# Three feature tiles a batch in the first edge pass, outputs from batch 18 on, the work between the layers in batches 25 to 51

## The reference

```
xn = layernorm(x)
def gat_conv(x, W, attn_l, attn_r):                  # H heads of D
    feat = (x @ W).reshape(n, H, D)
    el, er = (feat * attn_l).sum(-1), (feat * attn_r).sum(-1)
    e = leaky_relu(el[src] + er[dst], 0.2)
    ex = exp(e - segment_max(e, dst)[dst])
    return segment_sum(ex / segment_sum(ex, dst)[dst] * feat[src], dst)
gnn = gat_conv(elu(gat_conv(xn, W1, ...)), W2, ...)  # 8 heads of 64, then 1 head of 256

q, k, v = xn Wq, xn Wk, xn Wv                         # 8 heads of 32
q, k = elu(q) + 1, elu(k) + 1
mix = (q @ (k^T v)) / (q . sum(k)) @ Wproj + bproj    # linear attention over all nodes

x = x + gnn + mix
return x + experts(layernorm(x))                      # 8 experts, three products each, softmax gate
```

## Time and profile before

| | us |
|---|---|
| median of 3 runs | 3120.95 (3120.32 to 3121.43) |
| profiled execution | 3122.36 |
| its span | 3120.6 |
| busy in the span: PE, DVE, ACT, POOL | 2114.3, 2182.2, 1945.9, 2079.6 |

### The profile page before, as it was taken

One profiled execution on the slowest core, in us unless ns is written; L12 is line 12 of the kernel. 1 busy time (PEld: TensorE's weight loads), 2 busy tenths in 40 slices (PEclk: granted clock), 3 DMA queues, 4 the chain that ended last, 5 costly groups with the idle time before them and its releaser, 6 DMA issues. The chain is left out here.

```text
span 3120.6 us, 33304 instructions
## 1 busy us (share of the span) xinstructions
PE 2114.3 (68%) x7086; PEld 1324.1 (42%) x7086; DVE 2182.2 (70%) x5347; ACT 1945.9 (62%) x6385; POOL 2079.6 (67%) x1989
## 2 busy tenths in 40 slices
PE   6730455555555455657666101899999999999999
PEld 4520233333333333444444100565555555655565
DVE  7481799999998987888887245567666666666531
ACT  5610788888887677778776233566666666666532
POOL 4236777777777767777773477777777777777300
PEclk9965667667675566777676555999999999999999
DMA  7432899999999999999996377666666666666400
GB/s 231 133 56 70 316 372 368 380 379 371 372 358 375 369 356 325 335 334 331 343 325 214 104 233 233 196 214 207 220 200 213 215 212 211 219 207 212 140 21 13
DMA packets 242215, 779.00 MB, mean 250 GB/s; under 512 B 69152, under 2 KB 117109, under 8 KB 215357
## 3 DMA queue, kind: packets, MB, share of 16 engines
q0 software_dynamic: 124960, 364.74, 36.8%
q1 hardware_dynamic: 103886, 398.85, 34.3%
q10 hardware_dynamic: 13167, 13.29, 1.6%
HBM read 399.48 MB, written 378.12 MB: 249 GB/s over the span
## 5 line engine op out<-in xcount | busy, mean ns | idle before, releaser
L1910 POOL DMA_INDIRECT e_rows<-scratch_table,k_src x1664 | 1730.6, 1040 | 518.0 <-issue 354.0
L2043 ACT ACTIVATE e_rows<-e_rows 128x64 f32<-128x64 f32 (+1 forms) x4160 | 1193.7, 371 | 3.4
L2020 DVE SCALAR_TENSOR_TENSOR e_ring<-e_ring,k_same,e_rows 128x520 f32<-128x520 f32 (+1 forms) x1560 | 965.7, 619 | 267.0 <-ACT e_rows L2043 189.4
L2446 PE MATMUL e_p_y<-e_wfo,e_h 128*121 128x256 f32 x1664 | 388.2, 388 | 27.9 <-DVE e_y L2232 27.9
L2446 PEld LDWEIGHTS e_p_y<-e_wfo,e_h 128*121 128x121 f32 x1664 | 310.5, 188 | 123.6 <-issue 60.5
L2420 PE MATMUL e_p_a<-e_xt,e_wf 128*128 128x484 f32 x832 | 357.9, 573 | 0.7 <-ACT e_xt L2374 0.7
L2432 PE MATMUL e_p_b<-e_h,e_wf 128*128 128x484 f32 x832 | 357.3, 572 | 0.0
L2359 ACT ACTIVATE e_h<-e_p_a,e_shift,e_scale 128x484 f32<-128x484 f32 x208 | 154.8, 751 | 227.6 <-PE e_p_a L2420 227.4
L1115 PE MATMUL e_p_kv<-e_wkv,nd_feat 128*121 128x512 f32 x208 | 188.8, 1061 | 116.5 <-DVE nd_feat L1018 116.4
L2232 DVE SCALAR_TENSOR_TENSOR e_y<-e_p_y,e_w,e_y 121x256 f32<-121x256 f32 x416 | 180.8, 476 | 101.2 <-PE e_p_y L2446 100.9
L1989 DVE TENSOR_TENSOR e_rows<-e_rows,e_shared 128x4096 f32<-128x4096 f32 x52 | 229.7, 4418 | 21.3 <-ACT e_rows L2036 21.1
(11 more groups left out here) (426 smaller groups left out, 3325.2 us busy)
## 6 DMA issues: line engine op xcount, KB each, us to landing
scratch_rows_a<-e_ring SPq DMA_DIRECT2D x104, 2112.0 KB
scratch_rows_b<-e_ring SPq DMA_DIRECT2D x104, 1032.0 KB
e_rows<-scratch_table,k_src POOLq DMA_INDIRECT x1664
scratch_table<-na_frow ACTq DMA_DIRECT2D x52, 245.8 KB
scratch_table<-nd_feat SPq DMA_DIRECT2D x52, 124.8 KB
na_x<-in_x SPq DMA_DIRECT2D x13, 484.0 KB
e_wkv<-in_x SPq DMA_DIRECT2D x52, 121.0 KB
scratch_res<-e_wkv SPq DMA_DIRECT2D x52, 121.0 KB
```

The lines of the kernel that those rows point to most:

```text
L1910: nc.gpsimd.indirect_dma_start(out=rows[:, n % B, g, :], out_offset=None, in_=table, in_offset=bass.IndirectOffsetOnAxis(ap=k.src[:, n * G ...
L2020: nc.vector.scalar_tensor_tensor(ring[:, i, j - c0, 0:W + H], prev, k.same[:, n * G + j:n * G + j + 1], rows[:, rb, j, 0:W + H], ALU.mult, ...
L2043: last = nc.scalar.activation(rows[:, rb, j, at], rows[:, rb, j, at], ACT.Copy, scale=rows[:, rb, j, W + h:W + h + 1])
L2446: last = nc.tensor.matmul(self.p_y[bank][0:BK, i * D:(i + 1) * D], self.h2[:, e % 2, kt, v:v + BK], self.wfo[:, e, kt, :], start=kt == 0, ...
```

## The change

Features are worked out three tiles a batch in 18 batches (17 with three, the last with one); the outputs take batches 18 to 43, and batches 44 to 51 have neither features nor outputs. The work between the layers starts at batch 25 and has one or two tiles a batch, which start at steps 2 and 12 (in the last batch 2 and 7). The steps of the features move: ACT's parts stand after steps 2, 7 and 12, DVE's before steps 4, 9 and 14. The number of tiles of each kind is the same as before, and so are 46 tiles in the batches and six behind them.

```diff
-    HALF = NB // 2
+    EACH = 3
+    HALF = -(-NB // EACH)
+    OVER = HALF + NB // 2
...
     def tiles(self, n):
-        n = n % self.HALF
-        return (2 * n, 2 * n + 1)
+        if n < self.HALF:
+            return list(range(self.EACH * n, min(self.EACH * (n + 1), NB)))
+        n -= self.HALF
+        return [2 * n, 2 * n + 1] if n < NB // 2 else []
...
     def vector(self, dve, n, j):
-        t0, t1 = self.tiles(n)
         if n < self.HALF:
-            if j == 6:
-                self.features(dve, t0)
-            if j == 13:
-                self.features(dve, t1)
-        else:
+            for i, t in enumerate(self.tiles(n)):
+                if j == 4 + 5 * i:
+                    self.features(dve, t)
+        elif n < self.OVER:
+            t0, t1 = self.tiles(n)
...
     def scalar(self, act, n, j):
-        t0, t1 = self.tiles(n)
         if n < self.HALF:
-            if j == 4:
-                self.exponents(act, t0)
-            if j == 11:
-                self.exponents(act, t1)
-        else:
+            for i, t in enumerate(self.tiles(n)):
+                if j == 2 + 5 * i:
+                    self.exponents(act, t)
+        elif n < self.OVER:
+            t0, t1 = self.tiles(n)
...
             if n < self.HALF:
...
+                for i, t in enumerate(self.tiles(n)):
+                    self.project(pe, t)
+                    if i == 0 and q is not None:
+                        tails.tensor_turn(pe, q)
+                        tails.tensor_back(pe, q)
+                    if i == 0 and q1 is not None:
+                        tails.tensor_spread(pe, q1)
+                    if i == 1 and q is not None:
+                        tails.tensor_sum(pe, q)
+                    self.context(pe, t)
...
+START = Mixing.HALF + 7
...
-    FIRST = (33, 34, 35, 36, 37, 38, 40, 41)
-    TILES = {33: 1, 34: 2, 35: 2, 36: 3, 37: 3, 38: 2, 39: 3, 40: 3, 41: 2, 42: 3, 43: 3, 44: 2, 45: 3, 46: 3, 47: 2, 48: 3,
-             49: 2, 50: 2, 51: 2}
+    FIRST = tuple(START + i for i in (0, 1, 2, 3, 4, 5, 7, 8))
+    TILES = {n: 1 if (n - START) % 10 in (0, 4, 7) else 2 for n in range(START, NB)}
-    SLOT = [2 * i if n in (34, 35) else i for n, tiles in TILES.items() for i in range(tiles)]
+    SLOT = [(2 if n < NB - 1 else 1) * i for n, tiles in TILES.items() for i in range(tiles)]
...
-    OWN = 42
+    OWN = START + 9
```

More of the change, by code:

```diff
@@ L981, in sync @@
     def sync(self, sp, n, half):
-        t = self.tiles(n)[half]
         if half == 0:
@@ L986, in sync @@
             self.load_input(sp, half)
-        if n >= self.HALF:
+        if self.HALF <= n < self.OVER:
+            t = self.tiles(n)[half]
             sp.wait_ge(self.res_ready, t + 1)
@@ L1171, in tensor @@
             if n < self.HALF:
[L1172 to L1182, removed]
-            else:
-                self.weigh(pe, t0)
+                for i, t in enumerate(self.tiles(n)):
[8 more added lines that the diff above has]
+                    self.context(pe, t)
+            else:
+                tiles = self.tiles(n)
+                if tiles:
+                    self.weigh(pe, tiles[0])
                 hidden.transposes(pe, n - 1, 2)
@@ L1187, in tensor @@
                     tails.tensor_turn(pe, q)
-                self.turn_back(pe, t0)
+                if tiles:
+                    self.turn_back(pe, tiles[0])
                 if q1 is not None:
@@ L1192, in tensor @@
                     tails.tensor_back(pe, q)
-                self.output(pe, t0)
+                if tiles:
+                    self.output(pe, tiles[0])
                 hidden.product(pe, n - 1, 2)
-                self.weigh(pe, t1)
+                if tiles:
+                    self.weigh(pe, tiles[1])
                 hidden.transposes(pe, n, 0)
@@ L1198, in tensor @@
                     tails.tensor_sum(pe, q)
-                self.turn_back(pe, t1)
-                self.output(pe, t1)
+                if tiles:
+                    self.turn_back(pe, tiles[1])
+                    self.output(pe, tiles[1])
                 hidden.product(pe, n, 0)
@@ L1289, in __init__ @@
         self.late_ht = flat[:, at:at + 8 * BK].rearrange("p (i n) -> p i n", i=2)
-        assert (self.OWN - NB // 2) * 2 * 2 * BK >= at + 8 * BK
+        assert (self.OWN - Mixing.HALF) * 2 * 2 * BK >= at + 8 * BK
         self.place()
@@ L1343, in sync @@
         a, m = self.a, self.mixing
-        if n == 30:
+        if n == Mixing.HALF + 4:
             sp.wait_ge(m.ad_ready, self.free_tiles(4 * (D + 16) + 2 * D))
@@ L1453, in vector @@
     def vector(self, dve, n, j):
-        if n == 31 and j in (1, 2, 4, 6, 8):
+        if n == Mixing.HALF + 5 and j in (1, 2, 4, 6, 8):
             self.weights(dve, j)
```

## The result

The changed kernel takes 3207.36 us (median of 4 runs, 3204.18 to 3208.19) against 3121.19 for the kernel before beside it (4 runs, 3120.32 to 3121.64): a ratio of 1.0275, 95% interval 1.0257 to 1.0292. It is slower. The span of the profiled execution is 3206.4 us.

What follows compares the result with a forecast made beforehand. Bounds: POOL without free time in feature batches, and a DVE, PE, ACT loop around one feature tile. Stages 517 + 182 + 555 + 194 + 112 = 1560 us against 1466.5, +93.5, give 3214; range 3160 to 3250.

Steps and rivals of the forecast that it cites:

- 18 feature batches: Layer one's edge pass, batches 0 to 17: 17 x 29.0 + 24 = 517 us, replacing 615.7 but for eight batches less.
- outputs alone: Batches 18 to 24 repeat batches 26 to 32 of before, same parts and same place in the period: 182.0 us.
- hidden tiles alone: Batches 44 to 50: POOL issues 140 times, 197 us at 1.405 or 175 at 1.25; 194 taken, DVE waiting for rows.
- P: Time of PE's `project` for one feature tile: taken at 4.7 us, with 3.0 and 5.5 as ends.
- tight intervals: Times between successive L1018 in a feature batch, set by the DVE, PE, ACT loop: two a batch, P + 3.92 us each.
- period of four batches: Feature batches' recurring extras: 0.3 us for DVE's wait for ACT, 0.3 for scans, 0.8 for carries and merge, per batch.
- POOL cannot make it up: POOL's issues all remain, so waits in feature batches cannot be regained later: 17 x (29.0 - 23.7) = 90 us idle.
- The explanation by ports: Gathers take 0.94 us beside L1989, 1.42 beside L2020's two-SBUF-input sums; by that rule batches 44 to 50 cost 197 us.
- The third tile nearly free: Rival, feature batches: ACT does the third tile while it now waits for PE, 24.6 us a batch; 3105 us, 4%.
- The high clock: Rival, feature batches: PE's long rests go, a project takes 3.8 us, 27.2 a batch, the 18 take 486; 3183 us, 16%.
- POOL not binding behind the features: Rival, after the feature batches: hidden tiles alone cost 175 us, the batches before them 535; 3175 us, 14%.
- Slower still: Rival: P = 5.5 in feature batches (+27) and the output batches keep 30.8 us a batch (+30); 3271 us, 6%.

Runs made afterwards that it cites:

- The features alone: Kernel before with only three feature tiles a batch in batches 0 to 17, outputs and hidden tiles by the old table, batches 18 to 25 empty: 3206.22 us, ratio 1.0276.

## Why the prediction was right

The forecast was 3214 us, +93.5; it is 3207.4, +86. The terms, in its order:

| stage | predicted | measured |
|---|---|---|
| 18 feature batches | 517 | 512.0 |
| outputs alone | 182 | 184.6 |
| outputs and hidden tiles | 555 | 557.9 |
| hidden tiles alone | 194 | 188.1 |
| last batch and drain | 112 | 110.6 |

**Features: the mechanism is shown, the length of an ordinary batch within 1%.** An ordinary batch takes 28.85 us (17 of them 490.4) against 29.0, the last 21.6 against 24. Two steps inside it missed in opposite directions. P was taken at 4.7, and PE's groups of after give less (batches 1 to 17, 49 tiles):

```profile
L1117 PE MATMUL e_p_kv<-e_wkv,nd_feat 128*121 128x512 f32 x196 | 160.2, 964 | 66.5 <-DVE nd_feat L1022 66.5
L1120 PE MATMUL e_p_q<-nd_feat,e_early 128*128 128x121 f32 x392 | 63.4, 315 | 0.0
```

(160.2 + 63.4) / 49 - 0.20 = 4.36; single projects run from 2.9 to 5.5 us. The granted clock did rise, from 0.68 in the first 18 batches of before to 0.72. Against that, the 32 tight intervals of tiles 3 to 50 last 9.05 in the mean, not P + 3.92 = 8.3: the work on the carries between two features doesn't fall into spare time, as I took it to, but stands in the loop, as at 722.13 above. Without its project such an interval lasts 3.9 to 4.2 us in the two batches of a period that have no carries, 4.4 in the mean in the second, and 5.2 and 6.2 in the first. This is part of the 1.4 us that the forecast added for a period of four batches; by these means that part should have been 1.9 (28.85 - 18.2 - 2 x 4.36). That P was 0.34 too high, twice a batch, and this part 0.5 too low is luck: the two nearly cancel.

**POOL cannot make it up: right.** Predicted were 90 us of idle POOL, measured 99. Its gathers gave 14 back, which leaves 85: over 18 batches POOL is busy for 320.9 us instead of 335.0, since a gather takes 1.061 instead of 1.126 us when fewer begin inside a sum (80 of 281 issues in batches 1 to 17, 158 of 414 before). The features alone make the same loss, and eight empty batches cost 188 us.

**Outputs alone: 2.6 more than the 182.0 copied over.** The stage lasts as long as before within 1.5%; the copy was a fair price.

**Hidden tiles alone: the term that was mis-sized.** It was to be between POOL's 175 and 197, and I took 194. It is 188.1, since POOL's 143.4 and 129 gaps of 0.305 are 183 us. It issued 129 times there and not 140, because it used up a lead: in batch 44 its gathers started 4.4 us in the mean behind the sums that free their rows, in batch 49 it was 13.2. DVE's waits for rows, 9.5 us, come in batches 47 and 50 alone. The floor of issues was drawn from the first batch on, as if nothing had been ahead. The price of a gather in that stage, 1.095 us, is what the term said (1.10). The stages together were forecast 6.8 us too long, with errors of both signs.

**The explanation by ports.** The two rows that I weighed (0.94 beside L1989, 1.42 beside the sums) pointed the right way: the gathers stayed long with small stores and became short with short sums. By the rule of the Trainium skill ("SBUF — State Buffer", section "Who interferes with whom"), that a DVE instruction with two SBUF inputs contends with a GpSimd instruction that reads SBUF, the trace agrees: 157 of 158 gathers are held by a sum that they begin inside, and none of 76 by L1989. That a gather costs 1.42 beside sums was too simple, though, as not every gather beside them is held: it depends on how much of the sum is left when it begins. So a sum of 257 columns, which has two SBUF inputs as well, costs a gather almost nothing in the mean.

**The rivals.** The third tile nearly free (3105) is out in this kernel: its tight intervals last 7.4 to 10.2 us, 9.05 in the mean. It was also priced too low: with P = 3.0 the forecast's own terms give 18.2 + 6.0 + 1.4 = 25.6 us a batch, and the 24.6 that it uses has no working. With the second pair of tiles it is nearly free, and still gives no gain, since the balance point of 23.5 a batch is also POOL's price. The high clock (3183) was half true: P came down by 0.5 us of the 1.06 that it needed, and the carries in the loop took that back. POOL not binding behind the features (3175) took 175 and 535 for two stages that took 188.1 and 557.9; what spoke for it, that DVE was not seen to wait for rows, was wrong by two waits (7.1 and 6.2 us). Slower still (3271) needed P at 5.5.

## What to carry to other kernels

Where one engine's fixed work per batch fills the batch, packing other work into fewer batches saves nothing, because the emptied ones cost the same; it can only lose, if the packed ones become longer. Before work is packed, count the closed loops through a single buffer: with one PSUM pair a tile cost a whole round through DVE, PE and ACT (9 us), with two it cost nothing behind a full POOL, and the doubling is worth a try before the packing. To tell a full engine from one that merely keeps pace, add a known number of its smallest instructions: the run becomes longer by their price (1.25 us each) or not at all.

## What the runs showed of the hardware

- An indirect gather's issue on POOL takes 0.95 us and a fixed gap of 0.30 where no sum runs beside it. If it begins inside one of DVE's sums, which read two SBUF tiles, it ends 0.82 us after the end of that sum (157 of 158 with L2020 before, 80 of 80 with L2028 after, 42 of 43 with short sums), so it takes 0.95 to 1.5 us, in one case 2.05. Inside L1989, which reads one SBUF and one PSUM tile, it takes 0.95 (76 of 76).
- So the mean falls faster than the sum's length: with sums of 0.48 us instead of 0.75 fewer gathers begin inside one (43 of 398 issues in batches 2 to 25 against 158 of 414 in batches 1 to 25), and they find less of it left. Above 0.95 us the mean is 0.036 instead of 0.176.
- The size of the DMA traffic has no part in it: with the same sums 194 and 366 GB/s went with 1.117 and 1.126 us, and with short sums 394 GB/s with 0.986.
- A small gather (8 columns for each of 128 rows) costs POOL as much as one with 520: 1.077 us against 1.108 in the same batches of the kernel before. In the changed kernel it is 0.960 against 1.074; there 36 of 43 small ones overlap a sum by less than an eighth of their time.
